# One program for the delta rule and the gated output of a two-layer sequence kernel, with the first output group in the recurrence's last steps

## The reference

```
def step(S, inp):
    q_i, k_i, u_i, w_i = inp
    attn_i = jnp.where(lower_incl, q_i @ jnp.swapaxes(k_i, -1, -2), 0.0)
    u_adj = u_i - w_i @ S
    o_i = q_i @ S + attn_i @ u_adj
    S = S + jnp.swapaxes(k_i, -1, -2) @ u_adj
    return (S, o_i)
...
o = (1.0 - mix[..., None]) * o_d + mix[..., None] * ema_out
o = rms_norm(o, rms_w)
out = o.reshape(b, l, H * dv) @ Wo
...
def step(c, xt):
    ft = jax.nn.sigmoid(xt @ wf.T + c @ uf.T + bf)
    it = jax.nn.sigmoid(xt @ wi.T + c @ ui.T + bi)
    gt = jnp.tanh(xt @ wc.T + c @ uc.T + bc)
    c = ft * c + it * gt
    return (c, None)
c_final, _ = lax.scan(step, c0, x)
h = jnp.tanh(jnp.einsum('tbi,oi->tbo', x, wo) + c_final @ uo.T + bo)
```

## Time and profile before

| | us |
|---|---|
| median of 3 runs (1435.37 to 1441.69) | 1436.7 |
| the profiled execution | 1436.34 |
| its span in the trace | 1434.6 |
| PE busy in the span | 1277.0 (89%) |
| DVE, ACT, POOL busy in the span | 820.7, 463.3, 496.5 |
| TensorE's mean granted clock | 0.916 |

### The profile page before, as it was taken

How to read it: one execution, slowest core, us unless ns; L and a number is a source line. 1 busy time by engine, 2 the same in 40 slices (tenths; PEclk the granted TensorE clock), 3 DMA queues, 4 the chain that set the end, 5 groups by cost and what they waited for, 6 DMA issues and landing times. The chain is left out here.

```text
span 1434.6 us, 36334 instructions
## 1 busy us (share of the span) xinstructions
PE 1277.0 (89%) x12853; PEld 951.4 (66%) x12854; DVE 820.7 (57%) x1882; ACT 463.3 (32%) x1085; POOL 496.5 (35%) x709
## 2 busy tenths in 40 slices
PE   7999999899999999838888887298999999889997
PEld 5888888767776777614554555287888888746565
DVE  6788889533222222248888877457566666435443
ACT  1211222132222222226767774011222222123332
POOL 4344666415411111065666432223343434210000
PEclk9999999889999999968888997558999999779999
DMA  9999910113311211122444434612643334000001
GB/s 309 349 370 340 328 49 31 38 48 109 113 59 60 64 59 59 48 73 95 138 122 119 114 107 136 129 50 74 117 115 89 94 94 147 2 0 30 29 22 37
DMA packets 219962, 156.60 MB, mean 109 GB/s; under 512 B 111744, under 2 KB 201344, under 8 KB 219840
## 3 DMA queue, kind: packets, MB, share of 16 engines
q1 hardware_dynamic: 204288, 129.11, 30.7%
q0 software_dynamic: 9312, 25.44, 5.4%
q10 hardware_dynamic: 6240, 0.39, 0.3%
HBM read 64.47 MB, written 90.44 MB: 108 GB/s over the span
## 5 line engine op out<-in xcount | busy, mean ns | idle before, releaser
L945 PE MATMUL ps_sc<-w,a_qeo 128*128 x568 | 183.1, 466 | 0.0
L753 DVE TENSOR_TENSOR a_stm<-a_vpad,ps_sc 128x352 f32<-128x352 f32 x71 | 37.0, 521 | 177.2 <-ACT a_vpad L517 177.2
L945 PEld LDWEIGHTS ps_sc<-w,a_qeo 128*128 128x128 f32 x568 | 104.0, 193 | 46.5 <-issue 2.5
L423 POOL DMA_DIRECT2D x_slots<-a_stm x66 | 36.4, 551 | 226.1 <-issue 226.1
L1585 PE MATMUL d_pp<-d_xT,d_w_p 128*128 128x512 f32 x192 | 112.1, 732 | 1.1 <-ACT d_xT L1320 1.1
L1477 DVE SCALAR_TENSOR_TENSOR d_cout<-d_cin,d_taps,d_cout 128x512 f32<-128x512 f32 x144 | 106.1, 747 | 6.1 <-ACT d_cout L1338 2.7
L915 PE MATMUL ps_kv<-w,a_stm 128*128 x426 | 105.7, 384 | 1.2 <-DVE a_stm L746 1.1
L915 PEld LDWEIGHTS ps_kv<-w,a_stm 128*128 128x128 f32 x426 | 79.2, 190 | 30.1 <-issue 12.5
L2328 PE MATMUL g_pp<-g_xT,g_w_g 128*128 128x512 f32 x192 | 90.8, 613 | 8.3 <-ACT g_xT L2219 8.3
L1253 POOL DMA_INDIRECT got<-x_slots,d_idx x64 | 75.5, 1180 | 18.7 <-issue 16.1
L517 ACT ACTIVATE a_vpad<-ps_sc 128x352 f32<-128x352 f32 x71 | 33.0, 464 | 140.0 <-PE ps_sc L945 140.0
(11 more groups left out here) (273 smaller groups left out, 2834.4 us busy)
## 6 DMA issues: line engine op xcount, KB each, us to landing
x_slots<-a_zeros SPq DMA_DIRECT2D x32, 1024.0 KB, 11.0
rec<-d_kve SPq DMA_DIRECT2D x32, 384.0 KB, 2.9
u_kve<-rec SPq DMA_DIRECT2D x32, 384.0 KB, 3.9
a_qeo<-x_slots SPq DMA_DIRECT2D x71, 128.0 KB, 2.0
x_slots<-a_stm POOLq DMA_DIRECT2D x66, 128.0 KB, 2.1
rec<-d_act_out SPq DMA_DIRECT2D x32, 256.0 KB, 3.7
u_qkT<-rec SPq DMA_DIRECT2D x32, 256.0 KB, 3.5
w<-in_w SPq DMA_DIRECT2D x4, 1408.0 KB, 14.0
```

The source lines that it names most:

```text
L753: dve.tensor_tensor(e_h[:, q, 0:HID], e_gate[:, q, :], ps_3[q], ALU.mult).then_inc(h_out, 1)
L945: mm = pe.matmul(ps, e_xT[:, q, k, :], w13[:, s, k, bass.ds(e_hidden, 1), :], start=(k == 0), stop=(k == KD - 1))
```

## The change

`delta_rule` and `gated_output` become one function and one block, `rule_and_output`. The names of the gated output get the prefix `o_`. Its gate banks are the two banks of `u_bank_g`, which the recurrence last uses in step 32, and its output banks are two that the recurrence uses until its end; before the first output product PE waits for the recurrence's last results in them. `pipelined` gets an argument `after`, called behind each draining step with its number. Behind step 32, DVE and POOL do the moments, the root and the normalization of group 0. Behind step 33, the bias and uses 0 to 2 of group 0 follow on PE and ACT; behind steps 34, 35 and 36 uses 3 and 4, 5 and 6, and 7. All that comes later stands behind step 36 in the order that it had, from the moments of group 1 on. The steps of the groups are no longer a loop: all are written out.

```
-def pipelined(eng, n, depth, step, ahead=0, unroll=2, singly=0):
+def pipelined(eng, n, depth, step, ahead=0, unroll=2, singly=0, after=None):
...
     for i in range(hi, n + depth):
         step(i, i % unroll)
+        if after:
+            after(i)
...
+FIRST_USES = {NT + 1: (0, 1, 2), NT + 2: (3, 4), NT + 3: (5, 6), NT + 4: (7,)}
+GATE_LOADS = 16 * 11
...
+        o_pp = [b_g[:, e].rearrange("p z n t -> p (z n t)") for e in range(2)]
+        o_py = [b_ku, b_s]
...
+            pipelined(pool, NT, DEPTH, step, unroll=4, singly=GROUP * PART[1] + 1, after=lambda i: o_step(0, 0) if i == NT else None)
+            for i in range(1, NG + 2):
+                o_step(i, i % 2)
...
+            def o_first(i):
+
+                if i == NT + 1:
+                    act.wait_ge(o_bias_set, 4)
+                if i in FIRST_USES:
+                    o_step(1, 1, FIRST_USES[i])
...
+            def o_first(i):
+
+                if i == NT:
+                    o_step(0, 0)
+                if i == NT + 1:
+                    dve.wait_ge(gates_loaded, GATE_LOADS)
+                    dve.tensor_scalar(o_c0h[:, :], o_c0[:, :], 0.5, None, ALU.mult).then_inc(o_bias_set, 1)
+                    dve.wait_ge(o_bias_done, 1)
...
+                        if t == 0:
+                            pe.wait_ge(y_out, NT)
+                            pe.wait_ge(share_done, NT)
+                            pe.wait_ge(s_out, NT)
...
+            def o_first(i):
+
+                if i == NT + 1:
+                    pe.wait_ge(gates_loaded, GATE_LOADS)
+                    pe.wait_ge(stm_done, NT)
+                    pe.wait_ge(gu_done, NT)
+                    for n in range(3):
+                        for b in range(KD):
+                            for k in range(KD):
+                                mm = pe.matmul(o_pp[0][:, 2 * n + b:2 * n + b + 1], o_u_g[:, k, n, b * P:(b + 1) * P], o_c0[:, k:k + 1],
+                                               start=(k == 0), stop=(k == KD - 1))
+                    mm.then_inc(o_bias_done, 1)
+                    pe.wait_ge(o_bias_set, 4)
+                if i in FIRST_USES:
+                    o_step(1, 1, FIRST_USES[i])
+
+            pipelined(pe, NT, DEPTH, step, unroll=4, singly=GROUP * PART[1] + 1, after=o_first)
+            for i in range(2, NG + 2):
+                o_step(i, i % 2)
...
-        delta_rule(nc, kept, gate_kept, kept_loaded, got, l_in, l_back, t_sent, x_res, small, rec, l_mat, t_mat, w)
-        gated_output(nc, gate_kept, kept["ident"], kept_loaded, x_res, out)
+        rule_and_output(nc, kept, gate_kept, kept_loaded, got, l_in, l_back, t_sent, x_res, small, rec, l_mat, t_mat, w, out)
```

More of the change, by code:

```diff
@@ L1063, in load_gate_weights @@
     sp.dma_start(kept["b_o"][:, :], w["bo"].partition_broadcast(P)).then_inc(loaded, 16)
-    return 16 * 11
+    return GATE_LOADS
 def inverses_in(got):
@@ L1898, in step, with o_step, use @@
                     z.then_inc(s_out, 1)
-            pipelined(act, NT, DEPTH, step, unroll=4, singly=GROUP * PART[1] + 1)
+            def o_step(i, par, uses=range(8)):
+                u, q = i - 1, (par - 1) % 2
+                v = i - 2
+                def use(n):
+                    bank = o_pp[n % 2]
+                    act.wait_ge(o_p_done, 8 * u + n + 1)
+                    if n < 2:
+                        wait(act, o_y_done, GROUP * (u - 1))
+                        act.activation(o_xT[:, q, n, :], bank[:, :], ACT.Copy).then_inc(o_p_out, 1)
+                    else:
+                        b = n - 2
+                        wait(act, o_c_done, 2 * u)
+                        act.activation(o_gates[:, b, :], bank[:, :], ACT.Tanh, bias=o_bias[:, b:b + 1],
+                                       scale=0.5 if b < 4 else 1.0).then_inc(o_p_out, 1)
+                for n in uses:
+                    if has(u, NG):
+                        use(n)
+                    for j in o_AFTER[n] if has(v, NG) else ():
+                        t, s = GROUP * v + j, j % 2
+                        act.wait_ge(o_z_done, t + 1)
+                        wait(act, o_res_done, t - 1)
+                        act.activation(o_h[:, s, :], o_z[:, s, :], ACT.Tanh).then_inc(o_h_done, 1)
+            def o_first(i):
[3 more added lines that the diff above has]
+                    o_step(1, 1, FIRST_USES[i])
+            pipelined(act, NT, DEPTH, step, unroll=4, singly=GROUP * PART[1] + 1, after=o_first)
+            for i in range(2, NG + 2):
+                o_step(i, i % 2)
         @block.vector
@@ L1996, in _ @@
+            pipelined(dve, NT, DEPTH, step, unroll=4, singly=GROUP * PART[1] + 1, after=o_first)
+            for i in range(1, NG + 2):
+                o_step(i, i % 2)
         @block.tensor
```

315 lines of the change are left out of this document (125 added, 190 removed).

## The result

| | median us (runs) | lowest to highest | ratio to before, 95% interval |
|---|---|---|---|
| before | 1438.3 (22) | 1433.1 to 1442.6 | |
| changed | 1441.2 (22) | 1439.4 to 1445.5 | 1.0025, 1.0017 to 1.0032 |
| changed, a second time (beside 1434.0 us of before) | 1437.6 (11) | 1434.7 to 1438.4 | 1.0022, 1.0012 to 1.0032 |

The change makes the kernel slower by about 3 us, or 0.25%. That lies under the 0.5% that I had called the limit of a measurement, but so many runs tell it from nothing. The forecast was 1437 us, the profiled execution's 1436.34 plus 0.6, in a range from 1429.5 to 1444.

What follows compares the result with a forecast made beforehand. PE bounds the tail through its waits and low clock (11.1 us idle, granted clock 0.65). The terms move U by +0.6 us: 1434.6 + 0.6 + 1.74 = 1436.9, so 1437 us, range 1429.5 to 1444.

Steps and rivals of the forecast that it cites:

- step 33 (of it the gap for DVE): First recurrence step in the tail: group 0's moments and normalization on DVE cost PE 3.6 us, the lower clock 0.8 more.
- bias and DVE's part: Ahead of step 34: bias products 4.0 us, between 2.6 and 5.26, then 0.47 until DVE's two operations end.
- step 34: Recurrence step behind use 2 of group 0: kept at 10.0 us, 7.5 at the upper clock, 10.9 at the lower.
- uses 3 and 4: Group 0's gate products ahead of step 35: gapless, 4.9 us, between 3.43 and 6.86.
- wait behind them: PE's wait in step 35: ACT's last square queues behind use 4's tanh, so 3.5 us where it was 2.0.
- uses 5 to 7: Group 0's last gate products: 6.65 us, with 3.0 at the lower clock; 5.15 at the upper clock, 10.3 at the lower.
- tail: PE's stretch from step 33 to the end of use 7 of group 0; its end was to move +0.6 us.
- U: End of use 7 of group 0 on PE, the one number forecast: from 1280.15 to 1280.8, +0.6 us.
- The rival of a tail at the upper clock: Filled waits keep PE's clock up throughout the tail: U 10.7 us earlier, 1426 us; chance 0.17.
- the one that stays low: Gaps keep the tail at the lower clock: 8.4 us more than the forecast, 1445 us; chance 0.17.
- The rival of a middle gain, without the two queues: Square not behind the tanh, DVE's norm not holding L1934: 3.6 + 3.5 us of gaps go, 1430 us; no own chance.
- What I put at nothing: Barrier and branches (0.79 us on PE, within the old path), three waits ahead of the first output product, written-out groups: no effect.

Runs made afterwards that it cites:

- the merged kernel: Changed kernel with all of the first group moved back behind step 36, still one block: 1427.9 us, 0.9959; with DVE's bias ahead of group 0's moments: 1433.7 us, 0.9999.

## Why the prediction was right or wrong

It was right that the kernel hardly changes, and in the mechanism: both gaps are where it put them. How near it came is in part luck. Term by term, forecast against the changed kernel's trace:

| stretch of PE | forecast | measured |
|---|---|---|
| step 33 (of it the gap for DVE) | 15.5 (3.6) | 16.6 (3.85) |
| bias and DVE's part | 4.5 | 5.65 |
| transposes to use 2 | 2.72 | 2.75 |
| use 2 | 3.43 | 3.54 |
| step 34 | 10.0 | 9.8 |
| uses 3 and 4 | 4.9 | 4.3 |
| wait behind them | 3.5 | 3.37 |
| step 35 | 3.23 | 2.8 |
| uses 5 to 7 | 6.65 | 5.9 |
| tail | 54.4 | 54.7 |

The tail is off by 0.3 us, with errors of +2.4 and -2.1 us that cancelled. I had the bias at 4.0, between its prices at the two clocks, and it ran at the lower one throughout (5.12), while steps 34 and 35 and uses 3 to 7 saw more of the upper clock than I gave them. Step 33 cost 1.1 us more than forecast, as all that follows the gap in it ran at the lower clock: for that I had added 0.8 us, and PE's busy time in the step grew by 1.9 (12.21 against 10.33). PE's idle time in the tail is 10.7 us (54.67 - 43.99), forecast 10.4, before 11.1.

Of the signs that I had named, these came: L2035 late, the idle time, the wait of 3 to 4 us at the last tile's transposes, ended by DVE with ACT's square behind a tanh, and a clock between 0.55 and 0.8. The last tile's projection ends 22.6 us later, counted from step 33 (I had 20). U stands at 1281.6 and 1282.7 in two traces and at 1289.5 in the first, which the late start of step 33 explains. PE does not wait for DVE at group 1's first transposes.

What was off is the end from which it was counted. "U moves from 1280.15 to 1280.8" took the old tail from one trace, 53.7 us, where two others had 52.2. With the mean of the three, 52.7, the same sum gives +1.7 us, and the medians of the two comparisons gave 2.9 and 3.6. The three runs of before that were shown (1435.4 to 1441.7) could have warned me that one trace carries 1 or 2 us of luck.

The rival of a tail at the upper clock did not occur (0.69), nor the one that stays low. The rival of a middle gain, without the two queues, got no chance and was rightly left out for this kernel; as an experiment it gave more than its 7.1 us (12.5 by the ratios, 13.9 by the tails), since I had priced the gaps and not the clock that they take.

What I put at nothing, the barrier, the branches and the written-out groups, was nothing: with DVE's old order the merged kernel measured 0.9999. The hole is beside it. I never asked what the merged program would do with the first group left where it was. Moments ahead of the bias on DVE were worth 4 to 6 us, without any move. I had read the 5.15 us as part of the old path and not as an order on DVE. The change holds a gain of about 6 us and a loss of 7 to 9 us, and the sum of the whole path shows neither.

What stays open: what decides the moment at which the clock rises or falls. The traces show which stretches stood ahead of it, but the same work ran step 34 at 1.00 in one trace and at 0.68 in another, and the kernel before takes between 52.2 and 53.7 us for its tail.

## What to carry to other kernels

Before moving work into an earlier phase, look whether it is waiting for something that it doesn't need: here two independent pieces in the wrong order on DVE were the larger part of PE's wait between the bias and the first transposes, and exchanging them needs no move at all. (The exchange was measured in the merged program; in the kernel before it was not run.) When work is moved into a draining pipeline, put it where its engine already waits, and not between two steps: the same norm on DVE cost 6 us of step 33 ahead of the chain's first operation, and nothing in the wait 5 us later. On an engine that works in order, ask of each moved instruction which short one behind it starts a long path over other engines, and let that one pass.

## What the hardware showed that I had not expected

TensorE's clock makes gaps cost more than their length: taking two gaps of 3.85 and 3.37 us out saved 12.5 us by the ratios, and filling them with 22 products for nobody saved 5. It stood at 1.00 through both gaps, so what was lost was work at that level; behind the second it fell as well. The Trainium skill, "TensorE: Matmul & The Clock Gate", section "Loop structure matters more than you think", says that matmuls which follow immediately keep the engine warm. The traces agree from step 34 on with the filler (1.00), but not everywhere: 2.0 us into 24 products of one column without a gap the clock fell from 2.4 to 1.2 GHz ahead of step 33, and in every kernel whose step 33 was neither held nor behind the bias it fell within step 33, where the only gaps were 0.52 us ahead of products on 64 rows and 0.24 ahead of products on 32.

At the lower clock the same bias took 5.25 us in its own block and 5.12 in the merged one in every trace. Its 24 instructions of one column, 213 ns each, are as dear as 6 instructions of 512 columns there (seven filled 6.0 us).
